# Attention and mixture-of-experts block on one core: VectorE's routing and statistics cut into smaller pieces between its row maxima

## The chip, the core and the metric

The kernel runs on one core of a Trainium2 chip. It has five instruction queues: PE (TensorE, matmuls), DVE (VectorE), ACT (ScalarE), POOL (GpSimd) and SP (SyncE, which here only issues DMAs). They run side by side and meet at semaphores. Each queue is strictly in order, so an instruction that waits holds up everything behind it on its engine. The metric is the device time of one execution in microseconds (us); lower is better.

## The reference, cut to what matters

```python
x = x + layernorm(attn(layernorm(x)))      # x: (4, 1024, 128) f32, 16 heads of 8, causal
x = x + layernorm(ffn(layernorm(x)))
# attn: q, k, v from small projections with rotary terms, softmax(q k / sqrt(8), causal) v, then out @ wo + bo
# ffn, over xf = the 4096 rows:
xn = (xf - mu) * rsqrt(var + 1e-5) * ln_scale + ln_bias
probs = softmax(xn @ gate_w.T)             # 8 experts
tk_probs, tk_idx = top_k(probs, 2)
tk_probs = tk_probs / (sum(tk_probs) + 1e-5)
out = swiglu(xf, shared) + sum over the two picked experts of tk_prob * swiglu(xf, expert)
```

## The kernel before

There are three stages. The first makes q, k and v and stores them. The second, most of the first 600 us, is attention. The third runs the shared expert and the picked rows of the eight experts, tile by tile.

**Attention.** 4 batches x 16 heads are 64 heads, taken four at a time: 16 groups, g = 0 to 15, four groups to a batch. A group has 40 slots, numbered 0 to 39; in each slot PE makes one step of scores (`L2044`), and ACT takes their exponential (`expT`, `L1463`); every second slot PE also multiplies an earlier step by v (`L2017`). POOL blanks the diagonal blocks (`L1380`). There are three banks for scores, so PE can run at most three steps ahead of ACT.

**Row maxima.** The maximum of each row is needed one group ahead. PE makes the same scores a second time in the other orientation (`scores_for_max`, `L327`, `L334`), two banks at a time, and DVE reduces them (`maxima`, `L342`, written "block_max"): 18 such items for each group, spread over the slots. Two pairs of banks are used in turn: item p + 2 of the list `WIDE` may be written by PE only when DVE has read item p (`reuse`). After the 18th maximum DVE joins the pieces (`L1573` to `L1583`), POOL splits their negatives in three (`L1333` to `L1341`), PE turns them at slot 31 (`L1988`, the "neg" item), DVE copies them out (`negT`, `L1652`), and SP places them by DMA in the rows of q that the next group's first scores need.

**Side work.** While the four groups of a batch run, the batch before it (a "pair" q of two 512-row chunks; q = 0, 1, 2 during g = 4 to 15) passes through everything between attention and routing. `SIDE` gives the group in the batch (0 to 3) and the slot of what needs PE and a pair of banks; these items stand in `WIDE` between the maxima, and so take banks in turn with them:

- group 1: projection at slot 0; on DVE `proj_stats` of the two chunks at slots 6 and 12; POOL takes the root (`L759`); DVE's `shift` at slot 22, ACT normalizes.
- group 2: DVE adds the residual (`add_mid`), `mid_stats` at slots 4 and 8, `shift` and `row_var_of` at 20; ACT normalizes, PE turns the rows at slot 36 and ACT keeps them (`rows_turned`, `L802`).
- group 3: PE makes the two chunks' logits at slots 4 and 8 (`L990`); DVE scales them (`scaled`, `L876`) and, behind the second, runs the three instructions of `route1` (`L882` to `L886`); ACT takes the exponential at slot 12 (`exps`, `L806`); DVE then runs the 22 instructions of `route2_a` to `route2_d` in four runs at slots 15, 17, 20 and 22; PE makes `ranks` at slot 28, DVE finishes with `route3` (`L951` to `L959`); POOL scatters the rows from slot 32 on.

`stats` is three steps for one chunk: four BN_STATS, four BN_AGGR, one addition. Nearly every instruction of `stats`, `route1` and `route2` waits for a semaphore that the one before it raises. In the last group (g = 15) there are no maxima left, and the routing has slots of its own (`LAST_SIDE`, and the first tuple of `routes`).

The functions that the change touches, with the line numbers that the profile uses:

## Time and profile before

| | |
|---|---|
| median of 3 runs | 849.85 us (846.43 to 853.27) |
| the profiled execution | 846.51 us, its span 844.8 us |
| mean granted TensorE clock | 0.941 of full speed |
| PE / DVE / ACT / POOL busy | 694.6 / 603.4 / 504.1 / 323.1 us |
| row maxima on DVE | 288 of 1.22 us, 340.6 us busy |
| groups without side work (g = 1 to 3) | 26.7 us each |
| groups with side work (g = 4 to 14) | 28.3 to 34.8 us each |

A group is measured here from one copy of `negT` (slot 31) to the next. In a row of the timeline the columns are start, duration, engine, line, operation, what it writes and reads, and count; in brackets stands how long the engine was idle before it and what ended that. Instructions of one kind in a row are merged, and then the duration runs from the first start to the last end. An instruction may start a little before the one ahead of it ends.

### The profile page before, as it was taken

The numbers are of one execution on the slowest core, as the hardware profiler recorded it, in microseconds if no ns is written. First come the engines' busy times: TensorE is split into PE (matmuls) and PEld (weight loads), VectorE is DVE, ScalarE is ACT, GpSimd is POOL, SyncE is SP. The second block draws the span as 40 slices with busy tenths as digits, with TensorE's granted clock in tenths as the row PEclk, the third lists the DMA queues.
The fourth block names the chain that finished last, engine by engine and source line by source line (L and its number), as shares of the span: only waits on it lengthen the run. The fifth ranks groups of instructions, "written<-read, shape, count | busy, mean of one in ns | idle before, by whom it ended". The sixth has DMA issues, their size and how long they took to land.

```text
span 844.8 us, 17266 instructions
## 1 busy us (share of the span) xinstructions
PE 694.6 (82%) x6111; PEld 336.6 (40%) x6142; DVE 603.4 (71%) x1252; ACT 504.1 (60%) x1055; POOL 323.1 (38%) x437
## 2 busy tenths in 40 slices
PE   5887289999998898978888979879788856798886
PEld 2332023333343233323333324323277745677662
DVE  6899578888879888758888857886255552355465
ACT  3664056778777796666787656867655422244454
POOL 3775112212212321535231443433542244455574
PEclk9998589999999999989999989997999988899998
DMA  5456260121212213212123121007031121154264
GB/s 149 140 158 177 78 174 16 34 47 49 46 31 46 69 33 71 62 48 62 31 55 87 33 77 49 30 15 231 29 78 60 42 73 44 45 141 112 75 195 143
DMA packets 88784, 66.18 MB, mean 78 GB/s; under 512 B 27727, under 2 KB 75248, under 8 KB 88702
## 3 DMA queue, kind: packets, MB, share of 16 engines
q1 hardware_dynamic: 80076, 54.24, 24.8%
q0 software_dynamic: 4352, 8.99, 3.2%
q10 hardware_dynamic: 4274, 1.87, 0.9%
q8 instruction: 50, 0.82, 0.4%
q14 instruction: 32, 0.26, 0.1%
HBM read 38.11 MB, written 24.46 MB: 74 GB/s over the span
## 4 chain that ended last, share of the span: by engine, by line
PE 44%; DVE 20%; ACT 8%; issue 6%; another core or an unknown queue 4%; DMA 3%; SPq 2%; POOL 2%; ACTq 0%; DVEq 0%; POOLq 0%
DVE block_max L342 11%; PE ps L2017 10%; PE ps L2044 8%; PE ps L327 5%; PE ps L2124 4%; ACT expT L1463 4%; PE ps L334 2%; PE ps L1994 2%; SPq L1204 2%; PE ps L2113 2%; DMA q_space<-negT 2%; PE ps L2105 1%; PE ps L2082 1%; PE ps L2107 1%
## 5 line engine op out<-in xcount | busy, mean ns | idle before, releaser
L1463 ACT ACTIVATE expT<-ps 128x512 f32<-128x512 f32 (+1 forms) x640 | 325.3, 557 | 151.6 <-PE ps L2044 140.8
L342 DVE TENSOR_REDUCE block_max<-ps 128x8 f32<-128x1024 f32 x288 | 340.6, 1219 | 65.6 <-PE ps L327 44.6
L2017 PE MATMUL ps<-expT,vr 128*9 128x256 f32 (+1 forms) x2560 | 183.3, 368 | 16.2 <-ACT x_in L1423 12.6
L2044 PE MATMUL ps<-q_space,k_space 64*128 64x512 bf16 (+3 forms) x768 | 170.1, 340 | 15.7 <-DMA q_space<-negT 6.7
L327 PE MATMUL ps<-k_space,q_space 64*128 64x128 bf16 (+3 forms) x1152 | 135.3, 284 | 40.4 <-DVE block_max L342 24.2
L1380 POOL TENSOR_SCALAR_AFFINE_SELECT expT<-expT 128x512 f32<-128x512 f32 x128 | 83.8, 667 | 198.5 <-ACT expT L1463 198.4
L2044 PEld LDWEIGHTS ps<-q_space,k_space 64*128 64x128 bf16 x768 | 46.9, 94 | 163.7 <-ACT expT L1463 102.4
L1395 POOL DMA_INDIRECT expert_rows<-expT,tile_to x72 | 70.6, 980 | 91.3 <-ACT expT L1498 66.9
L327 PEld LDWEIGHTS ps<-k_space,q_space 64*128 64x128 bf16 x1152 | 50.8, 96 | 79.4 <-DVE block_max L342 55.9
L2017 PEld LDWEIGHTS ps<-expT,vr 128*9 128x9 f32 x2560 | 42.3, 89 | 98.9 <-issue 47.2
L1333 POOL TENSOR_SCALAR negs<-block_max 128x32 bf16<-128x32 f32 x16 | 4.7, 294 | 146.8 <-DVE block_max L1583 146.8
L2124 PE MATMUL ps<-w_gu,k_space 128*128 x288 | 44.1, 299 | 13.8 <-DVE k_space L1793 12.0
L1786 DVE TENSOR_TENSOR k_space<-k_space,ps 128x512 f32<-128x512 f32 x36 | 24.7, 687 | 42.3 <-remote 18.0
L771 POOL DMA_INDIRECT sorted_rows<-rows,places x48 | 47.0, 980 | 14.1 <-issue 12.3
L1498 ACT ACTIVATE expT<-ps,expT 128x128 f32<-128x128 f32 x72 | 22.5, 364 | 40.8 <-PE ps L2124 27.3
L2124 PEld LDWEIGHTS ps<-w_gu,k_space 128*128 128x128 f32 x288 | 37.5, 202 | 21.6 <-issue 21.4
L1490 ACT ACTIVATE k_space<-ps 128x512 f32<-128x512 f32 x36 | 21.5, 597 | 39.7 <-PE ps L2107 30.0
L1793 DVE COPY k_space<-ps 128x512 f32<-128x512 f32 x29 | 20.0, 691 | 34.1 <-PE ps L2113 19.1
L334 PE MATMUL ps<-later,identb 128*128 128x512 bf16 x97 | 33.5, 403 | 5.4 <-issue 5.4
L2113 PE MATMUL ps<-identf,k_space 128*128 128x128 f32 x144 | 22.9, 283 | 17.4 <-DVE k_space L1786 16.1
L2105 PE MATMUL ps<-w_hi,tile_hi 128*128 x72 | 35.4, 491 | 1.9 <-issue 1.6
L2107 PE MATMUL ps<-w_hi,tile_lo 128*128 x72 | 29.4, 408 | 0.0
(244 smaller groups left out, 953.0 us busy)
## 6 DMA issues: line engine op xcount, KB each, us to landing
expT<-sorted_rows SPq DMA_DIRECT2D x72, 65.0 KB
q_parts<-parts SPq DMA_DIRECT2D x24, 128.0 KB, 2.3
k_parts<-parts SPq DMA_DIRECT2D x24, 128.0 KB, 2.3
q_space<-q_parts SPq DMA_DIRECT2D x32, 96.0 KB
k_space<-k_parts SPq DMA_DIRECT2D x32, 96.0 KB
expT<-expert_rows SPq DMA_DIRECT2D x10, 256.0 KB, 4.2
v_ones<-v_st SPq DMA_DIRECT2D x8, 288.0 KB, 3.1
vr<-v_ones SPq DMA_DIRECT2D x16, 144.0 KB
```

The source lines that it names most:

```text
L327: last = nc.tensor.matmul(ps[:, 2 * odd + e, P * at:P * (at + n)], head_rows(qr, g, 2 * f + e, slice(qi * P, (qi + 1) * P)), head_rows(kr, ...
L334: last = nc.tensor.matmul(ps[:, 2 * odd + e], identb[:], later[:].rearrange("p n k -> p (n k)"), start=False, stop=True, skip_group_check= ...
L342: nc.vector.reduce_max(bm[:, g % 2, 2 * f:2 * f + 2, at:at + 4], ps[:, 2 * odd:2 * odd + 2].rearrange("p h (n k) -> p h n k", k=P), AX_X). ...
L771: nc.gpsimd.indirect_dma_start(out=xs_d, out_offset=bass.IndirectOffsetOnAxis(ap=pos[:, q, k, t:t + 1], axis=0), in_=xs(q)[:, t // NT, k, ...
L1380: nc.gpsimd.affine_select(out=tile, in_=tile, compare_op=ALU.is_ge, fill=0.0, base=0, pattern=[[0, GH], [1, P]], channel_multiplier=-1).th ...
L1395: nc.gpsimd.indirect_dma_start(out=y_d, out_offset=bass.IndirectOffsetOnAxis(ap=to[:, r, i:i + 1], axis=0), in_=yt[:, r, i], in_offset=Non ...
L1463: act.activation(expT[:, (NS * g + s) % PTN, hh, 0:width], ps[:, B_S + n % S_RING, 0:width], ACT.Exp, scale=SCALE).then_inc(exp_ok, 1)
L2017: last = nc.tensor.matmul(ps[32 * hh:32 * hh + VW, B_O, at:at + n], vr[:, g % RING, kt, hh * VW:(hh + 1) * VW], expT[:, (NS * g + s) % PTN ...
L2044: last = nc.tensor.matmul(ps[:, B_S + n % S_RING, col:col + m], head_rows(kr, g, hh, slice(kt * P, (kt + 1) * P)), head_rows(qr, g, hh, sl ...
L2105: nc.tensor.matmul(out, hi, wide_hi[:, bass.ds(at, 2 * INTER)], start=True, stop=False)
L2113: last = nc.tensor.transpose(ps[:, B_HT, P * i:P * (i + 1)], hu[:, u % 2, P * i:P * (i + 1)], identf[:])
L2124: last = nc.tensor.matmul(out, hT[:, q % 2, INTER * i + P * f:INTER * i + P * (f + 1)], wide_down[:, bass.ds(at + P * f, P)], start=f == 0 ...
```

## The change

`stats` takes a list of parts, and the three steps of a chunk stand two slots apart (6, 8, 10 and 10, 12, 14 in group 1; 4, 6, 8 and 8, 10, 12 in group 2). For the pairs q = 0 and 1, the logits move from slots 4 and 8 of the fourth group to slots 0 and 2, `route1`'s three instructions stand at slots 4, 6 and 8, ACT's exponential at slot 9 (before: 12), and `route2`'s 22 instructions stand one or two to a slot from 10 to 29. DVE takes `ranks` two slots later in its own order (30), while PE keeps it at slot 28. For q = 2 (g = 15) the routing's order is the same as before; its statistics in g = 13 and 14 are cut like the others. No instruction is added or taken away. The diff, with the bodies of the routing cut:

```diff
-SIDE = {"base": (0, 24), "turn": (0, 32), "project": (1, 0), "xf": (2, 36), "logits0": (3, 4), "logits1": (3, 8), "ranks": (3, 28), "count": (3, 30)}
-LAST_SIDE = {"logits0": (3, 0), "logits1": (3, 2), "ranks": (3, 13), "count": (3, 15)}
+SIDE = {"base": (0, 24), "turn": (0, 32), "project": (1, 0), "xf": (2, 36), "logits0": (3, 0), "logits1": (3, 2), "ranks": (3, 28), "count": (3, 30)}
+LAST_SIDE = {"ranks": (3, 13), "count": (3, 15)}
+ROUTED = {10: (0, 1), 12: (2, 3), 14: (4,), 15: (5,), 17: (6, 7), 19: (8, 9), 21: (10, 11), 23: (12, 13), 25: (14, 15), 27: (16, 17),
+          28: (18, 19), 29: (20, 21)}
...
+            if 0 in parts:
+                for t in range(NT):
+                    last = v.bn_stats(st[:, k, p, t], src[:, t])
+                last.then_inc(ln_ok[k], 1)
+            if 1 in parts:
+                dve.wait_ge(ln_ok[k], 3 * c + 1)
...
+            if 2 in parts:
+                dve.wait_ge(ln_ok[k], 3 * c + 2)
...
-                    if (r, slot) == (3, 4 if q == LAST - 1 else 12):
+                    if (r, slot) == (3, 4 if q == LAST - 1 else 9):
                         exps(act, q)
...
-                        route1(dve, g)
+                        if g == LAST - 1:
+                            route1(dve, g, range(3))
...
-                    if at == (1, 6):
-                        proj_stats(dve, 2 * q)
-                    if at == (1, 12):
-                        proj_stats(dve, 2 * q + 1)
+                    if g % NG == 1 and slot in (6, 8, 10):
+                        proj_stats(dve, 2 * q, (slot // 2 - 3,))
+                    if g % NG == 1 and slot in (10, 12, 14):
+                        proj_stats(dve, 2 * q + 1, (slot // 2 - 5,))
...
-                    if at == (2, 4):
-                        mid_stats(dve, 2 * q)
-                    if at == (2, 8):
-                        mid_stats(dve, 2 * q + 1)
+                    if g % NG == 2 and slot in (4, 6, 8):
+                        mid_stats(dve, 2 * q, (slot // 2 - 2,))
+                    if g % NG == 2 and slot in (8, 10, 12):
+                        mid_stats(dve, 2 * q + 1, (slot // 2 - 4,))
...
-                    routes = (5, 6, 8, 10) if q == LAST - 1 else (15, 17, 20, 22)
+                    if g % NG == NG - 1 and q < LAST - 1:
+                        if slot in (4, 6, 8):
+                            route1(dve, q, (slot // 2 - 2,))
+                        if slot in ROUTED:
+                            route2(dve, q, ROUTED[slot])
...
-                            if at == slot:
+                            if at + (2 if rest[0] == "ranks" and g < G - 1 else 0) == slot:
                                 item(p, *rest)
```

DVE's order at the first statistics, in g = 5 (a row is one kind of instruction, with its count; lines are each kernel's own). Before:

```order
L342 TENSOR_REDUCE block_max<-ps 128x2x4 x7
L827 BN_STATS stats<-q_space 128x6 x4
L831 BN_AGGR mean_var<-stats 128x2 x4
L834 TENSOR_SCALAR var_eps<-mean_var 128x4
L342 TENSOR_REDUCE block_max<-ps 128x2x4 x3
L827 BN_STATS stats<-q_space 128x6 x4
```

Now:

```order
L344 TENSOR_REDUCE block_max<-ps 128x2x4 x7
L830 BN_STATS stats<-q_space 128x6 x4
L344 TENSOR_REDUCE block_max<-ps 128x2x4
L835 BN_AGGR mean_var<-stats 128x2 x4
L344 TENSOR_REDUCE block_max<-ps 128x2x4
L839 TENSOR_SCALAR var_eps<-mean_var 128x4
L830 BN_STATS stats<-q_space 128x6 x4
```

A maximum now stands between each two steps, and the third step of the first chunk stands right ahead of the first step of the second.

DVE's order at the logits and `route1` in g = 7. Before:

```order
L342 TENSOR_REDUCE block_max<-ps 128x2x4 x6
L876 TENSOR_TENSOR logits<-ps,rstd_rows 128x32
L342 TENSOR_REDUCE block_max<-ps 128x2x4 x2
L876 TENSOR_TENSOR logits<-ps,rstd_rows 128x32
L882 TENSOR_TENSOR logits<-logits,base_logits 128x64
L884 TENSOR_REDUCE scalars<-logits 128x8
L886 TENSOR_TENSOR logits<-logits,scalars 128x64
L342 TENSOR_REDUCE block_max<-ps 128x2x4 x3
```

Now:

```order
L344 TENSOR_REDUCE block_max<-ps 128x2x4 x4
L883 TENSOR_TENSOR logits<-ps,rstd_rows 128x32
L344 TENSOR_REDUCE block_max<-ps 128x2x4
L883 TENSOR_TENSOR logits<-ps,rstd_rows 128x32
L344 TENSOR_REDUCE block_max<-ps 128x2x4
L891 TENSOR_TENSOR logits<-logits,base_logits 128x64
L344 TENSOR_REDUCE block_max<-ps 128x2x4
L894 TENSOR_REDUCE scalars<-logits 128x8
L344 TENSOR_REDUCE block_max<-ps 128x2x4
L897 TENSOR_TENSOR logits<-logits,scalars 128x64
```

The first scaling stands two maxima earlier, the second three, and `route1` is spread behind three maxima.

DVE's order at the end of the routing in the same group. Before:

```order
L342 TENSOR_REDUCE block_max<-ps 128x2x4 x2
L1658 RECIPROCAL rsum<-ps 128x16
L1661 TENSOR_TENSOR q_space<-ps,rsum 128x4x32
L951 TENSOR_TENSOR probs<-ps,tab 128x64
L954 TENSOR_TENSOR scratch<-onehot,probs 128x64
L955 TENSOR_TENSOR exps<-onehot,probs 128x64
L957 TENSOR_REDUCE places<-scratch 128x8
L959 TENSOR_REDUCE places<-exps 128x8
L342 TENSOR_REDUCE block_max<-ps 128x2x4
L1652 COPY negT<-ps 96x128
```

Now:

```order
L1684 RECIPROCAL rsum<-ps 128x16
L1687 TENSOR_TENSOR q_space<-ps,rsum 128x4x32
L957 TENSOR_SCALAR scalars<-scalars 128x8
L960 RECIPROCAL scalars<-scalars 128x8
L967 TENSOR_TENSOR rows<-scalars 128x2x4 x2
L344 TENSOR_REDUCE block_max<-ps 128x2x4
L976 TENSOR_TENSOR probs<-ps,tab 128x64
L979 TENSOR_TENSOR scratch<-onehot,probs 128x64
L980 TENSOR_TENSOR exps<-onehot,probs 128x64
L982 TENSOR_REDUCE places<-scratch 128x8
L984 TENSOR_REDUCE places<-exps 128x8
L1678 COPY negT<-ps 96x128
```

The last instructions of `route2` (the weights, `L957` to `L967`) now stand behind the output item (`rsum`), and the maximum of slot 29 has moved from behind `route3` to the place ahead of it. `seen`, which PE's `ranks` waits for, stands just ahead of it.

## Rows read from the trace of the kernel before

**Rows 1.** The page: busy time of the engines, and the chain that ended last.

```profile
PE 694.6 (82%) x6111; PEld 336.6 (40%) x6142; DVE 603.4 (71%) x1252; ACT 504.1 (60%) x1055; POOL 323.1 (38%) x437
...
PE 44%; DVE 20%; ACT 8%; issue 6%; another core or an unknown queue 4%; DMA 3%; SPq 2%; POOL 2%; ACTq 0%; DVEq 0%; POOLq 0%
```

**Rows 2.** Busy by engine from slot 31 to slot 31: g = 3, 5, 6, 7.

```profile
189.20:215.90 26.70, 24.99 (x299) 8.76 (x297) 22.93 (x29) 20.88 (x43) 6.33 (x13) 1.00 0.15 38
...
244.50:276.50 32.00, 29.04 (x325) 12.24 (x323) 26.02 (x49) 24.39 (x51) 8.35 (x15) 1.00 0.20 32
276.50:307.00 30.50, 26.10 (x299) 9.04 (x298) 27.46 (x55) 23.56 (x51) 10.71 (x18) 1.00 0.22 52
307.00:341.30 34.30, 30.47 (x336) 12.31 (x330) 28.80 (x62) 23.88 (x51) 6.34 (x13) 1.00 0.26 61
```

**Rows 3.** Timeline, DVE, logits and route1 in g = 7.

```profile
318.40 1.22 DVE L342 TENSOR_REDUCE block_max<-ps 128x8 f32<-128x1024 f32 x1 [0.89 <-PE ps L334]
320.04 1.23 DVE L342 TENSOR_REDUCE block_max<-ps 128x8 f32<-128x1024 f32 x1 [0.41 <-PE ps L334]
321.24 0.19 DVE L876 TENSOR_TENSOR logits<-ps,rstd_rows 128x32 f32<-128x32 f32 x1
321.47 0.26 DVE L882 TENSOR_TENSOR logits<-logits,base_logits 128x64 f32<-128x64 f32 x1
321.76 0.22 DVE L884 TENSOR_REDUCE scalars<-logits 128x8 f32<-128x64 f32 x1
322.01 0.23 DVE L886 TENSOR_TENSOR logits<-logits,scalars 128x64 f32<-128x64 f32 x1
322.15 3.48 DVE L342 TENSOR_REDUCE block_max<-ps 128x8 f32<-128x1024 f32 x3
```

**Rows 4.** Timeline, DVE, route3 and negT at the end of the same stretch.

```profile
338.46 0.25 DVE L1658 RECIPROCAL rsum<-ps 128x16 f32<-128x16 f32 x1
...
339.37 0.23 DVE L951 TENSOR_TENSOR probs<-ps,tab 128x64 f32<-128x64 f32 x1 [0.34 <-PE ps L1004]
...
340.17 1.21 DVE L342 TENSOR_REDUCE block_max<-ps 128x8 f32<-128x1024 f32 x1
341.30 0.21 DVE L1652 COPY negT<-ps 96x128 bf16<-96x128 bf16 x1
342.07 3.49 DVE L342 TENSOR_REDUCE block_max<-ps 128x8 f32<-128x1024 f32 x3 [0.56 <-PE ps L327]
```

**Rows 5.** Waits in g = 7: in total, times, longest, us.

```profile
PE ps L327 <- DVE block_max L342: 2.1, 3, 1.1
...
PE ps L1994 <- DVE block_max L342: 0.9, 1, 0.9
```

**Rows 6.** Timeline, DVE, first chunk's statistics in g = 5.

```profile
257.89 0.86 DVE L827 BATCH_NORM_STATS2 stats<-q_space 128x6 f32<-128x128 f32 x4
258.79 0.38 DVE L831 BATCH_NORM_AGGREGATE mean_var<-stats 128x2 f32<-128x6 f32 x4
259.20 0.23 DVE L834 TENSOR_SCALAR var_eps<-mean_var 128x4 f32<-128x4 f32 x1
259.34 3.47 DVE L342 TENSOR_REDUCE block_max<-ps 128x8 f32<-128x1024 f32 x3
```

**Rows 7.** Waits of PE in g = 5.

```profile
PE ps L327 <- DVE block_max L342: 1.4, 2, 0.9
```

**Rows 8.** Timeline, PE in g = 6, two maxima's scores behind statistics.

```profile
289.44 0.39 PE L327 MATMUL ps<-k_space,q_space 64*128 64x512 bf16 x2 [1.37 <-POOL expT L1380]
...
293.19 0.39 PE L327 MATMUL ps<-k_space,q_space 64*128 64x512 bf16 x2 [1.36 <-DVE block_max L342]
```

**Rows 9.** Timeline, ACT: turned rows ahead of g = 7, and its exponential.

```profile
311.39 1.12 ACT L802 ACTIVATE rows_turned<-ps 128x512 f32<-128x512 f32 x2
...
324.15 0.25 ACT L806 ACTIVATE exps<-logits 128x64 f32<-128x64 f32 x1
```

**Rows 10.** Timeline, PE: slot 0 of g = 7, and slot 0 of g = 8.

```profile
313.16 0.39 PE L2044 MATMUL ps<-q_space,k_space 64*128 64x512 bf16 x1
...
345.88 0.39 PE L2044 MATMUL ps<-q_space,k_space 64*128 64x512 bf16 x1 [0.43 <-DMA q_space<-negT]
```

More of the change, by code:

```diff
@@ L929, in route2_d @@
-        def route2_d(dve, q):
-            n = RT * q + R1
-            dve.wait_ge(rt, n + 16)
-            v.tensor_tensor(seen[:, q + 1], seen[:, q], sc[:, 6], ALU.add).then_inc(rt, 1)
-            v.tensor_tensor(sc[:, 7], sc[:, 2], sc[:, 4], ALU.add).then_inc(rt, 1)
-            dve.wait_ge(rt, n + 18)
-            v.tensor_scalar_add(sc[:, 7], sc[:, 7], EPS).then_inc(rt, 1)
-            dve.wait_ge(rt, n + 19)
-            v.reciprocal(sc[:, 7], sc[:, 7]).then_inc(rt, 1)
-            dve.wait_ge(rt, n + 20)
-            if q < PAIRS - 1:
-                wait(dve, sent, scattered(q))
-            for k in range(2):
-                v.tensor_tensor(xs(q)[:, :, k, :, COL_W],
-                                sc[:, 2 + 2 * k].rearrange("p (c t) -> p c t", c=2),
-                                sc[:, 7].rearrange("p (c t) -> p c t", c=2), ALU.mult).then_inc(rt, 1)
+            for i in ops:
+                if i == 0:
+                    dve.wait_ge(lg_ok, 2 * q + 2)
+                    v.tensor_tensor(lg[:], lg[:], base_lg[:].unsqueeze(1).to_broadcast([P, PAIR_T, NE]), ALU.add).then_inc(rt, 1)
+                if i == 1:
+                    dve.wait_ge(rt, n + 1)
+                    v.reduce_max(sc[:, 0], lg[:], AX_X).then_inc(rt, 1)
+                if i == 2:
+                    dve.wait_ge(rt, n + 2)
+                    v.tensor_tensor(lg[:], lg[:], each(sc[:, 0]), ALU.subtract).then_inc(rt, 1)
@@ L1765, in rows_stats @@
                     dve.wait_ge(projected, c + 1)
[L1766 removed]
+                    stats(dve, 0, c, ps[:, B_PROJ[c % 2]].rearrange("p (t e) -> p t e", e=E), range(3))
                 def keep_lo(q):
@@ L1863, in chain @@
                     if u == 4:
-                        mid_stats(dve, A)
+                        mid_stats(dve, A, range(3))
                         add_mid(dve, Z)
@@ L1867, in chain @@
                         shift(dve, 1, A)
-                        mid_stats(dve, Z)
+                        mid_stats(dve, Z, range(3))
                     if u == 6:
@@ L1874, in chain @@
                         scaled(dve, Z, B_ONE)
-                        route1(dve, LAST)
+                        route1(dve, LAST, range(3))
                     if u == 11:
-                        route2_a(dve, LAST)
+                        route2(dve, LAST, range(0, 5))
                     if u == 12:
-                        route2_b(dve, LAST)
+                        route2(dve, LAST, range(5, 10))
                     if u == 13:
-                        route2_c(dve, LAST)
+                        route2(dve, LAST, range(10, 16))
                     if u == 14:
-                        route2_d(dve, LAST)
+                        route2(dve, LAST, range(16, 22))
                     if u == 16:
```

162 lines of the change are left out of this document (93 added, 69 removed).

## The prediction

> **What bounds the kernel now.** I read the page's chain first, then a table of busy time cut at the copies of negT, then DVE's and PE's timelines inside the groups that the change touches. The chain runs over PE for 44% and over DVE for 20% [rows 1], so neither engine alone is the bound; where each one is must be read group by group. In a group without side work 26.7 us hold 25.0 us of PE and 22.9 us of DVE: PE leads. In g = 5, 6 and 7 the groups take 32.0, 30.5 and 34.3 us, and DVE has 26.0, 27.5 and 28.8 us of work in them [rows 2]. g = 9, 10, 11 repeat the three with the next pair, and g = 13 and 14 have the statistics too.
>
> DVE's timeline shows where in g = 7 it leads. Up to slot 8 it waits for PE: 0.89 us and 0.41 us ahead of the maxima at 318.40 and 320.04 [rows 3]. From 320.04 it runs without a stop, but for 0.34 us ahead of route3, to the copy of negT at 341.30 [rows 3, 4]; 21.3 us, from about slot 7 to slot 31. In that stretch PE waits for maxima to be read, 2.1 + 0.9 = 3.0 us in all [rows 5]. So in this stretch DVE is the bound, and each us that it loses there makes the group shorter, until PE's 3.0 us are used up. After the copy DVE waits for PE again, 0.56 us [rows 4]. The same pattern, shorter, surrounds the statistics: PE waits 1.4 us for DVE in g = 5 [rows 7] and 1.37 + 1.36 = 2.7 us in g = 6 [rows 8] (the first of these is put down to POOL, but it is a write into a pair of maxima banks behind a statistics run, where only DVE's reading can be late).
>
> **The change part by part.** No work is added or removed, so the sum is made of gaps and places.
>
> *Gaps behind a dependence.* In route1 an instruction that needs the one before it starts after that one's end: L884 at 321.76, 0.03 us after 321.47 + 0.26; L886 at 322.01, 0.03 after 321.76 + 0.22; L882 0.04 after L876. The maximum behind L886, which needs none of it, starts at 322.15, 0.09 us before 322.01 + 0.23 [rows 3]. The statistics say the same: BN_AGGR 0.04 after the end of BN_STATS, the addition 0.03 after BN_AGGR, the maximum 0.09 before the addition's end [rows 6]. A dependence costs 0.12 us, and a maximum of 1.22 us in between covers it whole.
> Statistics: two dependences in each of 12 chunk runs (2 in each of g = 5, 6, 9, 10, 13, 14) are covered: 24 x 0.12 = 2.9 us.
> Routing: route1's three. In route2 16 of the 21 neighbours were dependent and adjacent (4, 4, 5 and 3 in the four runs); now ten are (one inside each of the eight pairs (0,1), (2,3), (4,5), (6,7), (8,9), (10,11), (12,13), (14,15), and two along 18, 19, 20). 3 + 6 = 9 covered, 1.1 us in a group.
>
> The Trainium skill speaks against this term: the page "VectorE: DVE Perf Modes", section "The DRAIN you can't avoid", says that a chain of VectorE instructions takes the same time with a semaphore after each as without, so that one should count instructions and not semaphores. By that rule both terms above would be nothing and only what follows would be left. The 0.12 us between the two kinds of neighbours in rows 3 and 6 disagree, and I go by the rows.
>
> *route3.* Its 0.34 us wait for PE's ranks [rows 4] falls under the maximum that now stands ahead of it: 0.3 us in a group.
>
> *Work moved out of the full stretch.* The second scaling and route1 stood behind the first maximum of the stretch, at 321.24 to 322.15 [rows 3]. They now stand at slots 2 to 8, where DVE had 0.89 + 0.41 = 1.3 us to spare. Without their gaps four short instructions take 4 x 0.14 = 0.56 us (0.23 long, the next 0.09 early). 0.6 us in a group. PE makes the same logits, only sooner. What they need, the turned rows, is ready at 311.39 + 1.12 = 312.51 us and PE's slot 0 comes at 313.16 [rows 9, 10]: 0.65 us of cover. If that went, PE would stand, and the scores behind it.
>
> Per routing group 1.1 + 0.3 + 0.6 = 2.0 us, less than the 3.0 us that PE can give back; two groups (g = 7, 11) give 4.0. Each statistics group gives 0.48, less than 1.4 or 2.7. Together 2.9 + 4.0 = 6.9 us.
>
> *What gets tighter.* (a) ACT's exponential stands at slot 9, one slot behind the last of route1 at slot 8; before, ACT came to it at 324.15, nearly 2 us after route1's end at 322.24 [rows 3, 9]. ACT, in order, would hold its score exponentials behind it, and PE has three banks of scores to cover that. (b) PE's ranks at slot 28 need `seen`, which DVE now runs behind the maximum of slot 26, whose banks ranks must wait for anyway: 0.15 us more. (c) PE's neg at slot 31 takes the banks of ranks, so it waits for the first of route3; that now stands behind one more maximum (1.2 us). Counted from the end of the maximum of slot 26, near 338.46, negT was copied 2.8 us later [rows 4]; now `seen` and its neighbour 0.3, the output item 0.6, the four weight instructions 0.8, the maximum 1.1 and route3 0.8 come first, 3.6 us, of which 0.9 us stood ahead of that maximum before. So negT is no later, but PE stands before it. I put (a) to (c) at 0.5 us for a group, between 0 and, if each stall came in full (0.3, 0.2 and 1.3 us), 1.8 us. The statistics end two or four slots later than before, at slot 14 in the first of their groups and 12 in the second; DVE's shifts, which need POOL's root of them, stand at 22 and 20, eight slots on, so this costs nothing.
>
> The sum is 6.9 - 1.0 = 5.9 us at most likely values of its parts. It holds only if PE follows at once. PE waits for ACT too in these groups, and DVE's wait behind negT, 0.56 us, can grow by what DVE is early. I take eight tenths, 4.8 us. The profiled execution, 846.51 us, is 3.3 us under the median of its three runs, 849.85, which span 6.8 us by themselves. The profiled execution would come to about 841.7, the median to 845.0 us.
>
> **The rivals.**
> *A: PE takes most of it.* In g = 7 PE has 30.5 us of work in 34.3 us; while DVE keeps running, PE's own order and ACT might be right behind. Then the gaps close on DVE and open as waits of DVE for PE, and 0 to 2 us are left: 848 to 850. For it: DVE waits for PE on both sides of every full stretch. Against it: 3.0 us of PE's waits end at block_max.
> *B: slower.* PE standing at neg. The next group's first scores already wait 0.43 us for negT's DMA [rows 10], so there is no slack behind negT: each us that the copy comes later is a us on PE. If route3 behind the maximum of slot 29 makes PE turn the negatives late, by the 1.2 us of that maximum and as much again for the DMA and the scores that queue behind it, two groups lose some 2.5 us each, and if the gaps give nothing either the median is 849.9 + 5 = 855. It decides where route3's last four instructions (0.6 us) no longer cover PE's transpose: then DVE waits ahead of negT, and the copy comes more than 34 us after the one before.
> *C: the smoothing itself pays.* Runs of 1.5 us between maxima make PE stand in one piece; cut up, PE's two banks might cover them whole. If all waits of PE for maxima in the touched groups went, that is 2 x 3.0 + 3 x 1.4 + 3 x 2.7 = 18 us, 832 us. Against it: DVE runs without a stop through these stretches, and smoothing doesn't make its work less. For it: the idle time just ahead of each.
> *D: nothing moves,* as the skill's rule on semaphores would have it for the gaps, with the moved work (0.6 + 0.3 in two groups) eaten by the tighter places: 849 to 850.
>
> **How the numbers follow.** Forecast (3 to 7 us gained) 0.50; A and D together 0.27; B 0.11, most of it within 3 us; C, or half of C (9 to 18 us gained), 0.12. What a measurement can tell from no change is about 1%, 8.5 us: faster by more needs C or the best of the forecast with a lucky median, 0.14; slower by more needs B in full and more, 0.04; the same 0.82. The forecast's own range is 842 to 847. The range takes in A, D, half of B (+2.5) and half of C (-9), with the runs' own scatter: 839 to 852.
>
> **What would show it.** In the profile after: the copy of negT that ends g = 7 some 2 us sooner after the one that begins it (32 to 33 us for 34.3), g = 5 and 6 some 0.4 us shorter each; on DVE, BN_AGGR starting 0.09 us before the end of a maximum; in g = 7 PE's waits for block_max down from 3.0 to about 1 us. Wrong would be: a new wait of ACT for route1's last instruction, of PE at neg or at the logits, DVE idle inside the stretch from slot 8 to 31, or g = 7 at 34 us with DVE's waits for PE grown by what the gaps gave.

## The result, and the profile after

| | before | changed |
|---|---|---|
| median of 11 runs each | 849.85 us (845.74 to 854.48) | 843.24 us (838.34 to 849.16) |
| ratio | | 0.9929, 95% interval 0.9902 to 0.9956 |
| the profiled execution, its span | 846.51, 844.8 us | 844.97, 843.2 us |
| forecast | | 845.0 us, range 839 to 852 |

By the ratio the change takes 6 us off, between 3.7 and 8.3. The experiments below ran on other chips, where the kernel before took 843 to 847 us; each is set against the kernel before beside it, and their times aren't comparable with those of this table. The two profiled executions differ by only 1.6 us, so their spans can't be compared as they stand; cut into groups they can. A group's length, from one copy of negT to the next, in us:

| g | 1 to 3 | 5 | 6 | 7 | 8 | 9 | 10 | 11 | 12 | 13 | 14 |
|---|---|---|---|---|---|---|---|---|---|---|---|
| touched | no | statistics | statistics | routing | no | statistics | statistics | routing | no | statistics | statistics |
| before | 26.7 | 32.0 | 30.45 | 34.3 | 34.1 | 32.4 | 30.5 | 34.8 | 34.6 | 32.4 | 28.3 |
| changed | 26.7 | 31.6 | 29.4 | 33.8 | 35.2 | 31.7 | 29.5 | 33.8 | 34.7 | 31.6 | 27.4 |

The six statistics groups lose 4.9 us, the two routing groups 1.5, together 6.4, which is near the gain of the medians. What hides it between the two profiles lies where both kernels are the same: 2.1 us more before g = 4, 1.1 in g = 8 and 1.5 behind g = 14. g = 8 and 12 came out between 33.2 and 35.6 us in the runs below whatever was changed. Their granted clock was 0.85 to 0.90, and PE's longest wait in them, 2.9 to 3.8 us in g = 8 here, is one for which the profile names no releaser; the code has PE wait there for a group's rows. Groups 1 to 3 came out at 26.65 to 26.8 wherever nothing was added to them.

Two things stay open. Over all traces here the seven kernels with spread routing have g = 8 and 12 at 34.7 us on average and those with the routing in runs, `paired` and the disturbed g = 12 of `probe` left out, at 34.3; that is within the scatter, but it could take back part of what the routing gives. And g = 9 took 32.4 us, as before, in two other traces with the changed statistics (`mix` and `ranks28`), so 0.7 of the 4.9 us isn't there in every execution; g = 5, 6, 10, 13 and 14 repeat within 0.12 us in the traces with these statistics.

The same four windows as [rows 2], and g = 11; the columns are stretch, length, then busy time (and instructions) of PE, weight loads, DVE, ACT, POOL, then granted clock, DMA share and GB/s:

```profile
246.67:278.23 31.56, 29.08 (x325) 12.20 (x323) 25.73 (x50) 24.41 (x51) 8.41 (x15) 1.00 0.18 32
278.23:307.67 29.44, 26.07 (x299) 9.03 (x297) 26.88 (x54) 23.52 (x51) 10.77 (x18) 1.00 0.23 54
307.67:341.43 33.76, 30.10 (x336) 12.26 (x330) 28.30 (x61) 24.32 (x51) 6.37 (x13) 1.00 0.26 62
...
437.78:471.56 33.78, 30.10 (x336) 12.26 (x330) 28.32 (x61) 24.33 (x51) 6.37 (x13) 1.00 0.24 61
```

g = 11 of the kernel before had a granted clock of 0.95, not 1.00:

```profile
438.22:472.99 34.77, 31.65 (x336) 12.62 (x330) 28.96 (x61) 23.89 (x51) 6.34 (x13) 0.95 0.25 60
```

In runs below that keep the old routing, g = 11 took 34.3 to 34.6 us at full clock. Like with like, the routing is worth 0.5 us in g = 7 and 0.5 to 0.9 in g = 11.

**Statistics.** DVE in g = 6 of the changed kernel:

```profile
288.46 0.86 DVE L830 BATCH_NORM_STATS2 stats<-x_rows 128x6 f32<-128x128 f32 x4
289.24 1.21 DVE L344 TENSOR_REDUCE block_max<-ps 128x8 f32<-128x1024 f32 x1
290.36 0.37 DVE L835 BATCH_NORM_AGGREGATE mean_var<-stats 128x2 f32<-128x6 f32 x4
290.65 1.19 DVE L344 TENSOR_REDUCE block_max<-ps 128x8 f32<-128x1024 f32 x1
291.76 0.16 DVE L839 TENSOR_SCALAR var_eps<-mean_var 128x4 f32<-128x4 f32 x1
```

Behind the four BN_STATS the next instruction now starts 0.78 us after the first of the four, where BN_AGGR started 0.90 after it [rows 6]; behind BN_AGGR 0.29 for 0.41. The gaps are gone, 0.12 us each. And PE in the same group, where [rows 8] had two waits of 1.37 and 1.36 us:

```profile
290.50 0.39 PE L329 MATMUL ps<-k_space,q_space 64*128 64x512 bf16 x2 [0.75 <-POOL expT L1405]
291.90 0.39 PE L329 MATMUL ps<-k_space,q_space 64*128 64x512 bf16 x2 [0.24 <-DVE block_max L344]
293.87 0.39 PE L329 MATMUL ps<-k_space,q_space 64*128 64x512 bf16 x2 [0.71 <-DVE block_max L344]
```

1.70 us for 2.73: 1.03 us less, as the group is 1.0 us shorter.

**Routing.** DVE in g = 7, the counterpart of [rows 3]:

```profile
315.63 0.18 DVE L883 TENSOR_TENSOR logits<-ps,rstd_rows 128x32 f32<-128x32 f32 x1
316.21 1.23 DVE L344 TENSOR_REDUCE block_max<-ps 128x8 f32<-128x1024 f32 x1 [0.40 <-PE ps L329]
318.28 0.19 DVE L883 TENSOR_TENSOR logits<-ps,rstd_rows 128x32 f32<-128x32 f32 x1 [0.84 <-PE ps L1015]
318.82 1.22 DVE L344 TENSOR_REDUCE block_max<-ps 128x8 f32<-128x1024 f32 x1 [0.34 <-PE ps L329]
319.96 0.21 DVE L891 TENSOR_TENSOR logits<-logits,base_logits 128x64 f32<-128x64 f32 x1
320.24 1.23 DVE L344 TENSOR_REDUCE block_max<-ps 128x8 f32<-128x1024 f32 x1
321.38 0.21 DVE L894 TENSOR_REDUCE scalars<-logits 128x8 f32<-128x64 f32 x1
321.88 1.23 DVE L344 TENSOR_REDUCE block_max<-ps 128x8 f32<-128x1024 f32 x1 [0.29 <-PE ps L336]
323.02 0.54 DVE L897 TENSOR_TENSOR logits<-logits,scalars 128x64 f32<-128x64 f32 x1
```

Here DVE now waits four times for PE, 0.40 + 0.84 + 0.34 + 0.29 = 1.87 us, where it waited 0.89 + 0.41 [rows 3]. It is full (never waits for another engine) only from 321.88, 14.2 us after the copy that opens the group; before it was from 320.04, 13.05 us after. At the other end:

```profile
339.51 1.23 DVE L344 TENSOR_REDUCE block_max<-ps 128x8 f32<-128x1024 f32 x1
340.65 0.21 DVE L976 TENSOR_TENSOR probs<-ps,tab 128x64 f32<-128x64 f32 x1
...
341.43 0.21 DVE L1678 COPY negT<-ps 96x128 bf16<-96x128 bf16 x1
342.31 3.48 DVE L344 TENSOR_REDUCE block_max<-ps 128x8 f32<-128x1024 f32 x3 [0.67 <-PE ps L329]
```

the 0.34 us ahead of route3 [rows 4] are gone. And the waits, the counterpart of [rows 5]:

```profile
DVE block_max L344 <- PE ps L329: 4.0, 7, 1.0
...
PE ps L2025 <- DVE block_max L344: 0.8, 1, 0.8
PE ps L2019 <- DVE probs L976: 0.6, 1, 0.6
...
ACT exps L808 <- DVE logits L897: 0.4, 1, 0.4
...
PE ps L329 <- DVE block_max L344: 0.2, 1, 0.2
```

PE's waits for maxima to be read fell from 3.0 to 1.0 us. Two new waits are those that the prediction named: 0.58 us of PE at the negatives and 0.36 us of ACT at the exponential. A third it didn't name: PE now waits 0.56 and 0.60 us, before 0.24 in all, at the products behind ACT's copy of half a group's output (the profile writes "x_in"):

```profile
322.83 0.62 PE L2048 MATMUL ps<-expT,vr 128*9 128x256 f32 x8 [0.56 <-ACT x_in L1448]
...
330.96 0.62 PE L2048 MATMUL ps<-expT,vr 128*9 128x256 f32 x8 [0.60 <-ACT x_in L1448]
```

Over all causes PE's waits in g = 7 fell only from 3.7 to 3.5 us.

### The profile page after: what moved, and what is told of

Same layout as the page of the kernel before. It is cut to its first block, busy times and chain, and to the rows that moved or that the text cites. A ratio compares the mean times of both kernels' runs of the same rounds, so it can differ in the third digit from the quotient of the medians.

```text
span 843.2 us, 17266 instructions
## 1 busy us (share of the span) xinstructions
PE 696.8 (83%) x6111; PEld 334.3 (40%) x6142; DVE 600.3 (71%) x1252; ACT 504.1 (60%) x1055; POOL 323.8 (38%) x437
## 3 DMA queue, kind: packets, MB, share of 16 engines
q10 hardware_dynamic: 4274, 1.87, 0.8%
## 4 chain that ended last, share of the span: by engine, by line
PE 45%; DVE 20%; ACT 7%; issue 6%; another core or an unknown queue 4%; DMA 3%; SPq 2%; POOL 2%; ACTq 0%; DVEq 0%; POOLq 0%
DVE block_max L344 11%; PE ps L2048 11%; PE ps L2075 9%; PE ps L329 5%; PE ps L2155 4%; ACT expT L1488 4%; PE ps L336 2%; SPq L1229 2%; PE ps L2144 2%; PE ps L2025 2%; DMA q_space<-negT 2%; PE ps L2136 1%; PE ps L2137 1%; PE ps L2138 1%
## 5 line engine op out<-in xcount | busy, mean ns | idle before, releaser
L2048 PE MATMUL ps<-expT,vr 128*9 128x256 f32 (+1 forms) x2560 | 185.9, 373 | 17.5 <-ACT x_in L1448 15.9
L329 PE MATMUL ps<-k_space,q_space 64*128 64x128 bf16 (+3 forms) x1152 | 137.5, 286 | 31.7 <-DVE block_max L344 16.4
L2155 PE MATMUL ps<-w_gu,k_space 128*128 x288 | 44.0, 299 | 14.2 <-DVE k_space L1824 11.3
L1824 DVE COPY k_space<-ps 128x512 f32<-128x512 f32 x29 | 20.0, 691 | 33.3 <-PE ps L2144 21.7
L2137 PE MATMUL ps<-w_lo,tile_hi 128*128 x72 | 29.6, 411 | 0.0
```

The lines of the kernel that those rows point to most:

```text
L329: last = nc.tensor.matmul(ps[:, 2 * odd + e, P * at:P * (at + n)], head_rows(qr, g, 2 * f + e, slice(qi * P, (qi + 1) * P)), head_rows(kr, ...
L2048: last = nc.tensor.matmul(ps[32 * hh:32 * hh + VW, B_O, at:at + n], vr[:, g % RING, kt, hh * VW:(hh + 1) * VW], expT[:, (NS * g + s) % PTN ...
L2155: last = nc.tensor.matmul(out, hT[:, q % 2, INTER * i + P * f:INTER * i + P * (f + 1)], wide_down[:, bass.ds(at + P * f, P)], start=f == 0 ...
```

## The experiments

### The two halves of the change, apart

`stats_only` has the statistics of the changed kernel and the routing of the one before; `routing_only` the reverse. The edit of `routing_only` against the changed kernel, its first half (the statistics of the second group are put back in the same way):

```diff
-                    if g % NG == 1 and slot in (6, 8, 10):
-                        proj_stats(dve, 2 * q, (slot // 2 - 3,))
-                    if g % NG == 1 and slot in (10, 12, 14):
-                        proj_stats(dve, 2 * q + 1, (slot // 2 - 5,))
+                    if at == (1, 6):
+                        proj_stats(dve, 2 * q, range(3))
+                    if at == (1, 12):
+                        proj_stats(dve, 2 * q + 1, range(3))
...
```

`stats_only` undoes in the same way what `old_front` and `old_runs` below undo apart.

Expected of the first:

> Only the statistics are cut in three, the routing stands as in the kernel before. If each part of the change acts in its own groups, g = 5, 6, 9, 10, 13, 14 keep the lengths that the changed kernel showed (31.6, 29.4, 31.7, 29.5, 31.6, 27.4 us, 4.9 us less in all than before) and g = 7 and 11 go back to 34.3 and 34.8: time about 845 against 850, ratio 0.994. If the gain were the routing's, the ratio would be 1.00.

Expected of the second:

> Only the routing is spread and moved, the statistics are whole again. Parts that act apart: g = 7 at 33.8 and g = 11 at 33.8 us, the statistics' groups as before, 1.6 us less in all, ratio 0.998. By the prediction's sum the two groups would give 4 us, ratio 0.995, with the statistics' cutting only hiding it; the changed kernel's trace speaks against that.

Measured: `stats_only` 837.49 us against 842.98 for the kernel before on the same chip, ratio 0.9946 (0.9913 to 0.9978), with g = 5, 6, 9, 10, 13, 14 at 31.5, 29.4, 31.6, 29.4, 31.5, 27.4 us and g = 7 back at 34.3. `routing_only` 842.97 us, ratio 0.9997 (0.9959 to 1.0035), with g = 7 at 33.8 us and the statistics' groups as before. Its g = 11 took 36.4 us at a granted clock of 0.91. The parts act each in its own groups; the statistics carry most of the gain, and what the routing gives by its two groups, 1.0 to 1.4 us, is less than these timings can tell from nothing.

### The routing's front and back, apart

`old_front` is the changed kernel with the logits at slots 4 and 8, route1 in one run and the exponential at slot 12; `old_runs` keeps the early front and puts route2 back in its four runs.

```diff
-SIDE = {"base": (0, 24), "turn": (0, 32), "project": (1, 0), "xf": (2, 36), "logits0": (3, 0), "logits1": (3, 2), "ranks": (3, 28), "count": (3, 30)}
+SIDE = {"base": (0, 24), "turn": (0, 32), "project": (1, 0), "xf": (2, 36), "logits0": (3, 4), "logits1": (3, 8), "ranks": (3, 28), "count": (3, 30)}
-ROUTED = {10: (0, 1), 12: (2, 3), 14: (4,), 15: (5,), 17: (6, 7), 19: (8, 9), 21: (10, 11), 23: (12, 13), 25: (14, 15), 27: (16, 17),
+ROUTED = {13: (0, 1), 14: (2, 3), 15: (4, 5), 17: (6, 7), 19: (8, 9), 21: (10, 11), 23: (12, 13), 25: (14, 15), 27: (16, 17),
...
-                    if (r, slot) == (3, 4 if q == LAST - 1 else 9):
+                    if (r, slot) == (3, 4 if q == LAST - 1 else 12):
...
-                        if g == LAST - 1:
-                            route1(dve, g, range(3))
+                        route1(dve, g, range(3))
...
-                        if slot in (4, 6, 8):
-                            route1(dve, q, (slot // 2 - 2,))
```

> The changed kernel with the logits at slots 4 and 8, route1 in one run and ACT's exponential at slot 12 as in the kernel before; route2's 22 instructions stand between the maxima from slot 13 on (four of them together at slots 14 and 15). If the early logits make PE the bound in slots 0 to 9 and so take the gain of the moved work, g = 7 is no longer than the 33.8 us of the changed kernel, perhaps 33.5. If moving route1 into DVE's idle time is worth its 0.6 us, g = 7 is 34.4 us.

```diff
-ROUTED = {10: (0, 1), 12: (2, 3), 14: (4,), 15: (5,), 17: (6, 7), 19: (8, 9), 21: (10, 11), 23: (12, 13), 25: (14, 15), 27: (16, 17),
-          28: (18, 19), 29: (20, 21)}
+ROUTED = {15: tuple(range(5)), 17: tuple(range(5, 10)), 20: tuple(range(10, 16)), 22: tuple(range(16, 22))}
-                            if at + (2 if rest[0] == "ranks" and g < G - 1 else 0) == slot:
+                            if at == slot:
```

> The changed kernel's logits, route1 and exponential, but route2 in its four runs at slots 15, 17, 20 and 22, and route3 at slot 28. By the prediction's sum, g = 7 loses the 0.7 us of gaps and the 0.3 us of route3's wait: 34.8 us. If only the moved work counts, it stays at 33.8; if the early front is worth nothing, it is 34.3 as before.

| front | back | kernel | g = 7 | ratio |
|---|---|---|---|---|
| old | old | `stats_only` | 34.29 us | 0.9946 (0.9913 to 0.9978) |
| early | old | `old_runs` | 34.94 us | 0.9938 (0.9909 to 0.9968) |
| old | spread | `old_front` | 33.25 us | 0.9924 (0.9889 to 0.9959) |
| early | spread | changed | 33.76 us | 0.9929 (0.9902 to 0.9956) |

The four lengths add up: spreading route2 and route3 is worth 1.0 us with the old front and 1.2 with the early one, and the early front costs 0.65 us with the old back and 0.5 with the spread one; 1.1 and 0.6 below. The ratios are too close to tell these apart; the groups are not, since g = 7 was at full clock in all four. DVE's waits show where the 0.6 us go. In `old_front` they are those of [rows 3] again:

```profile
316.72 1.23 DVE L344 TENSOR_REDUCE block_max<-ps 128x8 f32<-128x1024 f32 x1 [0.89 <-PE ps L336]
318.36 1.23 DVE L344 TENSOR_REDUCE block_max<-ps 128x8 f32<-128x1024 f32 x1 [0.42 <-PE ps L336]
```

1.31 us against the changed kernel's 1.87, with its 0.32 us longer L897 on top: 0.9 us more, less 0.36 us of route1's gaps: 0.5.

### Route3 back at slot 28 on DVE

```diff
-          28: (18, 19), 29: (20, 21)}
+          28: (18, 19, 20, 21)}
-                            if at + (2 if rest[0] == "ranks" and g < G - 1 else 0) == slot:
+                            if at == slot:
```

> The changed kernel, but DVE takes route3 at slot 28 as PE does, behind the four weight instructions, and the maximum of slot 29 stands behind it. PE's wait of 0.58 us at the negatives goes and DVE's wait of some 0.3 us ahead of route3 comes back. If the late route3 is worth what the prediction's sum says, g = 7 is 34.1 us for 33.8; if PE's wait at the negatives matters more, 33.6.

Measured, in one execution: 843.89 us, against 846.55 in one of the kernel before beside it; g = 11 took 33.72 us at full clock, against the changed kernel's 33.78. (g = 7, of which the expectation spoke, took 35.2, but ran at a granted clock of 0.87 for 13 us from 306.80 on, so its length says nothing.) In g = 11 PE's wait at the negatives went and nothing came in its place:

```profile
469.47 0.25 DVE L967 TENSOR_TENSOR rows<-scalars 128x8 f32<-128x8 f32 x2
469.63 0.22 DVE L976 TENSOR_TENSOR probs<-ps,tab 128x64 f32<-128x64 f32 x1
...
471.55 0.21 DVE L1678 COPY negT<-ps 96x128 bf16<-96x128 bf16 x1
472.12 1.23 DVE L344 TENSOR_REDUCE block_max<-ps 128x8 f32<-128x1024 f32 x1 [0.36 <-PE ps L329]
```

DVE doesn't wait ahead of route3 even here: the four weight instructions that now stand behind `seen` cover PE's ranks. So the 0.3 us of route3's wait were saved by the place of the weight instructions, not by the two slots. Neither branch of the expectation (0.3 us longer, 0.2 us shorter) came; by this one group the late route3 is worth nothing.

### What a dependence costs, and what a full stretch passes on

`probe` is the kernel before, with instructions added on DVE that nothing needs:

```diff
+                    if g == 1 and slot == 12:
+                        for i in range(8):
+                            chained(i)
+                    if g == 2 and slot == 12:
+                        dve.wait_ge(pbs, 9)
+                        for i in range(8):
+                            last = v.tensor_tensor(pb[:, i], base_tab, base_tab, ALU.mult)
+                        last.then_inc(pbs, 1)
+                    if g == 3 and slot in (12, 14, 17, 19, 21, 23, 25, 29):
+                        i = (12, 14, 17, 19, 21, 23, 25, 29).index(slot)
+                        dve.wait_ge(pbs, 10 + i)
+                        v.tensor_tensor(pb[:, i % 2], pb[:, (i + 1) % 2], base_tab, ALU.mult).then_inc(pbs, 1)
...
+                        v.tensor_tensor(wide[:, at % 3], w_gu[:, at], w_gu[:, at + 1], ALU.mult).then_inc(pbs, 1)
```

> The kernel before, with small instructions added on DVE that nothing needs: in g = 1 eight of 128x64 that each need the one before, in one run at slot 12; in g = 2 eight like them that need nothing, in one run; in g = 3 eight dependent ones each behind a maximum. In g = 7 three of 128x512 (0.69 us) at slots 14, 18 and 23, inside the stretch where DVE never waits; in g = 11 the same three at slots 34, 36 and 38, where DVE waits for PE. If a dependence costs 0.11 to 0.12 us and a full stretch passes DVE's time on, the starts in g = 1 are 0.25 us apart and in g = 2 0.13 us, g = 7 grows by 1.8 us to 36.1, and g = 12, which begins at slot 31 of g = 11, by much less than that. If semaphores cost nothing, both spacings are the same.

One execution took 851.99 us, against 846.55 of the kernel before beside it. DVE's timeline in g = 1 (a chain), g = 2 (the same eight without one) and g = 3 (a chain, one to a place):

```profile
150.69 2.03 DVE L1713 TENSOR_TENSOR shared<-shared 128x64 f32<-128x64 f32 x8
...
178.64 1.16 DVE L1722 TENSOR_TENSOR shared<-shared 128x64 f32<-128x64 f32 x8
...
205.72 0.21 DVE L1727 TENSOR_TENSOR shared<-shared 128x64 f32<-128x64 f32 x1
205.85 1.22 DVE L342 TENSOR_REDUCE block_max<-ps 128x8 f32<-128x1024 f32 x1
```

With 0.21 us for the last one, the starts of the chain are (2.03 - 0.21) / 7 = 0.26 us apart and those of the others (1.16 - 0.21) / 7 = 0.14: a dependence costs 0.12 us. The groups, 26.7 us without the additions, took 28.0, 27.1 and 26.7. These are groups with 3.8 us of DVE to spare, and still the chain in one run cost 1.3 us and the run of eight others 0.4, while eight dependent instructions at eight places cost nothing. PE shows why, in g = 1 and g = 2:

```profile
153.91 0.39 PE L327 MATMUL ps<-k_space,q_space 64*128 64x512 bf16 x2 [1.21 <-DVE block_max L342]
...
180.99 0.39 PE L327 MATMUL ps<-k_space,q_space 64*128 64x512 bf16 x2 [0.33 <-DVE block_max L342]
```

In g = 3, and in the same groups of the kernel before, PE has no wait for a maximum at all. A run makes PE stand, and that time isn't made up for by DVE's time to spare. In g = 7 three instructions of 0.69 us, 2.06 us in all, made the group 36.3 for 34.3 us: the full stretch passes DVE's time on nearly one to one. (The granted clock fell to 0.56 for 6 us near its end, but DVE's waits add up to 4.6 us as before, so PE's slower clock seems to have stayed hidden behind DVE.) The same three behind slot 31 of g = 11 left that group at 34.3 us; g = 12, where they count, took 35.6, but varies as much by itself, so that part tells nothing.

### Covered but in one run; cut but not covered

`paired` puts both chunks' statistics in one run in which each dependence is covered by the other chunk's step. `halves` cuts each chunk's in two through its BN_STATS and leaves both dependences adjacent. Both keep the routing of the kernel before; their edits on the statistics' places:

```diff
+                    if at == (1, 12):
+                        pair_stats(dve, 0, q, [at_rows(2 * q), at_rows(2 * q + 1)], proj_kept)
...
+                    if at == (2, 8):
+                        pair_stats(dve, 1, q, [x_rows[:, 0], x_rows[:, 1]], mid_ok)
...
```

> Routing as before. The statistics of both chunks stand in one run of six steps at slot 12 of their first group and slot 8 of the second (all BN_STATS, all BN_AGGR, both additions), so each of the four dependences is covered by the other chunk's step, and no maximum stands between. If covered dependences are all that the cutting gives (0.48 us a group), g = 5 and 6 are 31.5 and 30.0 us, as short as or shorter than the length before (32.0, 30.5). If the cutting works by keeping PE from standing behind a long run, the run of 2.6 us makes them as long as before or longer: 32 to 33 and 30.5 to 31.5.

```diff
+                    if g % NG == 1 and slot in (6, 8):
+                        proj_stats(dve, 2 * q, {6: (9,), 8: (0, 1, 2)}[slot])
+                    if g % NG == 1 and slot in (12, 14):
+                        proj_stats(dve, 2 * q + 1, {12: (9,), 14: (0, 1, 2)}[slot])
...
+                    if g % NG == 2 and slot in (4, 6):
+                        mid_stats(dve, 2 * q, {4: (9,), 6: (0, 1, 2)}[slot])
+                    if g % NG == 2 and slot in (8, 10):
+                        mid_stats(dve, 2 * q + 1, {8: (9,), 10: (0, 1, 2)}[slot])
```

> Routing as before. Each chunk's statistics are cut in two pieces, two BN_STATS and then, two slots on, the other two with BN_AGGR and the addition; so runs are shorter, but both dependences stay adjacent. If only covered dependences count, g = 5 and 6 stay at 32.0 and 30.4 us. If shorter runs count, they fall toward the 31.5 and 29.4 of the run with the statistics alone, g = 6 to about 29.9.

| statistics | covered | longest run | g = 5 | g = 6 | g = 10 |
|---|---|---|---|---|---|
| before | no | 1.5 us | 32.0 | 30.45 | 30.5 |
| `paired` | yes | 2.4 us | 32.0 | 32.0 (clock 0.89) | 31.35 (clock 0.95) |
| `halves` | no | 1.0 us | 31.2 | 30.0 | 30.0 |
| changed | yes | 0.9 us | 31.6 | 29.4 | 29.5 |

`paired` (one execution, 858.65 us, at a mean granted clock of 0.915, where all other profiles had 0.934 to 0.941, so its time says little) has 0.5 us less for DVE to do in each of these groups. g = 5, at full clock throughout, is not shorter for it: PE stands once for 1.55 us. In g = 10 PE stands for 1.93 us, and behind the run DVE waits 2.03 us for PE where it had been full:

```profile
423.46 1.63 DVE L845 BATCH_NORM_STATS2 stats<-x_rows 128x6 f32<-128x128 f32 x8
425.01 0.63 DVE L850 BATCH_NORM_AGGREGATE mean_var<-stats 128x2 f32<-128x6 f32 x8
425.55 0.29 DVE L854 TENSOR_SCALAR var_eps<-mean_var 128x4 f32<-128x4 f32 x2
425.75 3.48 DVE L343 TENSOR_REDUCE block_max<-ps 128x8 f32<-128x1024 f32 x3
431.26 0.26 DVE L1698 RECIPROCAL rsum<-ps 128x16 f32<-128x16 f32 x1 [2.03 <-PE ps L2033]
```

```profile
427.03 0.39 PE L328 MATMUL ps<-k_space,q_space 64*128 64x512 bf16 x2 [1.93 <-DVE block_max L343]
```

Part of that second wait is the clock's, which fell behind PE's wait (last section), so g = 6 and 10 show more than a long run alone. `paired` also moves the first chunk's statistics to the second's slot, so place and length aren't told apart in it. What it was to tell is that covered dependences in one run gain nothing anywhere.

`halves` (one execution, 845.56 us, against 846.55 of the kernel before beside it) covers no dependence and still takes 0.8 us off g = 5 and 0.45 off g = 6. So both causes are real and of one size in g = 6: 0.45 us from shorter runs, and the other 0.55 of the changed kernel's 1.0 once the gaps are covered as well (predicted for them: 0.48). In g = 5 and 9 the run's length and place matter more: `halves` has both at 31.2 us, below the changed kernel's 31.6 and 31.7. In g = 13 it doesn't, 32.0 against 31.65.

### A version with the better halves, and two finer ones

`best` takes `old_front`'s routing, two pieces in the first statistics group and three in the second. `mix` puts the logits at slots 2 and 6 with route1 spread behind them; `fine` is `mix` with each chunk's statistics in four pieces. Of each edit the lines that set the places:

```diff
+                    for i, at_slot in enumerate(({6: (9,), 8: (8, 1, 2)}, {12: (9,), 14: (8, 1, 2)})):
+                        if g % NG == 1 and slot in at_slot:
+                            proj_stats(dve, 2 * q + i, at_slot[slot])
```

> The routing of the run with the old front (g = 7 and 11 at 33.2 and 33.3 us), statistics in three steps in the second group (29.4 us) and in two pieces in the first (31.2 us for 31.6). If each part acts in its own group, it is 1.1 to 1.2 us for both routing groups below the changed kernel and 0.4 us for each of g = 5, 9, 13: together 2.3 us below the changed kernel, 8 to 8.5 us below the kernel before, ratio 0.990.

```diff
-SIDE = {"base": (0, 24), "turn": (0, 32), "project": (1, 0), "xf": (2, 36), "logits0": (3, 4), "logits1": (3, 8), "ranks": (3, 28), "count": (3, 30)}
+SIDE = {"base": (0, 24), "turn": (0, 32), "project": (1, 0), "xf": (2, 36), "logits0": (3, 2), "logits1": (3, 6), "ranks": (3, 28), "count": (3, 30)}
+                        if slot in (7, 9, 11):
+                            route1(dve, q, (slot // 2 - 3,))
```

> The run with the old front, but the logits at slots 2 and 6, route1's three instructions at slots 7, 9 and 11 behind maxima, and ACT's exponential still at slot 12. If only the logits' two matmul runs close together at the head of the group cost the changed kernel its 0.6 us, spreading route1 gains here: g = 7 at 32.9 us for 33.2. If moving any of it ahead of the stretch in which DVE is full starves DVE the same way, g = 7 is 33.5 us or more.

```diff
+                    for i, at_slot in enumerate(({6: (9,), 8: (8,), 10: (1,), 12: (2,)}, {12: (9,), 14: (8,), 17: (1,), 19: (2,)})):
...
+                    for i, at_slot in enumerate(({4: (9,), 6: (8,), 8: (1,), 9: (2,)}, {9: (9,), 11: (8,), 12: (1,), 14: (2,)})):
```

> The run before in this call (logits at 2 and 6), with the statistics cut in four pieces for each chunk, two BN_STATS at most between maxima. If shorter runs keep paying, g = 5 is 31.0 us or less for 31.2 and g = 6 29.1 for 29.4; if what is left is DVE's work itself, they stay at 31.2 and 29.4.

| | median | before beside it | ratio | g = 5 | g = 6 | g = 7 |
|---|---|---|---|---|---|---|
| `best` | 839.61 | 846.21 | 0.9918 (0.9889 to 0.9947) | 31.2 | 29.5 | 33.3 |
| `mix` | 843.46 | 846.21 | 0.9963 (0.9934 to 0.9993) | 31.5 | 29.4 | 33.7 |
| `fine` | 841.52 | 846.21 | 0.9951 (0.9924 to 0.9977) | 30.8 | 29.5 | 33.8 |

`mix` would have had g = 7 at 32.9 us if the closeness of the two logits were what costs; it took 33.7, as if any move ahead of the full stretch costs the same. Between the two copies DVE waits 4.8 us for PE in it, as in the changed kernel, and 4.25 in `old_front`:

```profile
318.47 0.19 DVE L883 TENSOR_TENSOR logits<-ps,rstd_rows 128x32 f32<-128x32 f32 x1 [0.63 <-PE ps L1015]
319.56 1.22 DVE L344 TENSOR_REDUCE block_max<-ps 128x8 f32<-128x1024 f32 x1 [0.64 <-PE ps L336]
```

`fine` gains another 0.4 us in g = 5 (30.8) and nothing in g = 6. But its g = 9 and 13, which have the same edit as g = 5, took 31.9 and 32.0 us, 0.25 and 0.35 more than in the changed kernel, so shorter runs than the changed kernel's aren't shown to pay. `best` has the touched groups 1.7 us below the changed kernel's (246.9 against 248.7 us for the eight, before 255.1; 2.3 were expected, and most of the difference is g = 13, which stayed at 31.6), but its ratio can't be told from the changed kernel's. It beats the kernel before; that it beats the changed one rests on the groups of one execution alone.

## Why the prediction was right, and where it wasn't

**The time** came out at 843.24 against 845.0, inside the range, and the 1% bound held: the same, by the text's own measure. The 4.8 us forecast are 6 us by the ratio and 6.4 us by the groups. But two of its terms were wrong by nearly the same amount, some 2 us, in opposite directions, so that the time came out so near is in part luck. (Eight tenths of 5.9 are 4.7 and not 4.8 us, which changes nothing.)

**Gaps behind a dependence: right.** 0.12 us from rows 3 and 6, 0.12 from the probe. The Trainium skill's page "VectorE: DVE Perf Modes", section "The DRAIN you can't avoid", found eight copies to take the same time with a semaphore after each as with one after the last; for 128x64 instructions that need each other the probe's 2.03 against 1.16 us for eight say otherwise. A wait on something long done cost nothing: the probe's eight dependent instructions at eight places left g = 3 at 26.7 us.

**Statistics: 2.9 us predicted, 4.9 measured.** The step that failed is the case against rival C: "DVE runs without a stop through these stretches, and smoothing doesn't make its work less". DVE's work isn't less, but the stretch in which it is full has two ends. When a run makes PE stand, PE comes out of the stretch later, and DVE then waits for it; a shorter run lets PE follow, and the waits beyond the stretch shrink. `halves`, which covers nothing, shows it at 0.8 us in g = 5 and 0.45 in g = 6 and 10, and g = 5 of `paired` in reverse: 0.5 us less work, and no gain. I had counted those waits of DVE (0.55 us at g = 6's end before, 0.22 after) as fixed. The rival in full, 18 us, was far off: PE's waits in g = 6 went from 2.7 to 1.7 us, not to none.

**Routing: 2.0 us a group predicted before its deductions, 0.5 measured in g = 7.** By parts, from the four lengths of g = 7:
- gaps and route3's wait: `old_front` covers five dependences, 0.6 us, and route3's wait, 0.3, together 0.9 us; it measured 1.0. Right, but for the reason given for route3's wait, which by `ranks28` is the weight instructions' place.
- work moved out of the full stretch, +0.6 us: measured, with route1's covered gaps, -0.6 us. This is the step that failed: "PE makes the same logits, only sooner". Each chunk's logits take PE 1.06 us. At slot 8 they fell where DVE was about to have all it could do; at slot 2 they fall where DVE has nothing else to read, and it waits 0.84 us for them and more for the maxima behind. I looked at what DVE could do in its idle time and not at who made it idle: it was waiting for PE, and PE got more to do first. The account closes: between the two copies DVE's waits grew from 4.6 to 4.8 us, its work and gaps fell from 29.7 to 28.95. Nor was "less than the 3.0 us that PE can give back" a bound that held: PE's waits for maxima did fall by 1.9 us, but 0.9 us came back as waits for ACT and 0.8 at ranks and the negatives.
- tighter places, 0.5 us: PE waits 0.58 us at the negatives, 0.20 at ranks and ACT 0.36 at the exponential, as named. What they cost the group is little: without the first, g = 11 is 0.06 us shorter.

**The rivals.** A happened in the routing's front, at that place only. B didn't: negT is not later, and the next group's first scores wait 0.32 us for its DMA, before 0.43 [rows 10]. C is right in kind, a part of the gain does come from the smoothing, and a tenth in size: 2 of 18 us. D is ruled out by the statistics.

**What it said would show it:** PE's waits for block_max at 1 us came true, but g = 7 at 32 to 33 us was wrong (33.8), and two of its own signs of failure are in the trace, PE's wait at neg and ACT's for route1's last instruction; DVE's waits for PE grew too, by 0.2 us; g = 5 and 6 "some 0.4 us shorter each" was right for the first and half for the second.

## What to carry to other kernels

Side work on an engine that another engine waits for is worth cutting until no run makes the other engine stand; here that paid even where both engines have idle time, and without less work. A dependence between small neighbouring VectorE instructions cost 0.12 us here, and nothing once a maximum stood between them. Before moving work into an engine's idle time, ask which engine made it idle: if the move gives that one something to do first, the idle time can grow, as it did here.
